# A shared tile's columns: from TensorE transposes to loads in 32x32 blocks and a VectorE transpose

## The chip, the cores and the metric

The kernel runs on one core of a Trainium2 chip. The metric is the device time of one execution in microseconds (us). All arithmetic is fp32; matmuls run on fp32 numbers split into a high and a low part (type fp32r), so that three matmuls of parts stand for one.

## The reference

`x` is (128, 64, 256): 128 samples of 64 rows of 256 numbers. Two stages, each added to its input.

```python
# stage 1, per sample b with type itok[b] (one of the five experts):
s0 = relu(x @ swi[0]) @ swo[0];  s1 = relu(x @ swi[1]) @ swo[1]        # shared, 256 -> 1024 -> 256
eo = relu(x @ wi[itok]) @ wo[itok]                                     # the sample's expert
w  = softmax(relu(concat(eo[:, 0], s0[:, 0], s1[:, 0]) @ g1) @ g2)     # from row 0 of each sample
x  = x + eo * w[:, 0] + s0 * w[:, 1] + s1 * w[:, 2]
# stage 2, a reaction-diffusion step on each sample's 64 x 256 grid, edges reflected:
x  = x + zX * (left - 2x + right) + zY * (up - 2x + down) + zR * x * (1 - x)
```

## The kernel before

**Passes.** The work is cut into passes of 8 chunks (a chunk is 128 of the 1024 hidden columns). Two `PRE` passes compute s0 and s1 for row 0 of each sample, 21 `EXP` passes the experts (a unit is 8 samples with one expert, for 14 big units, or 4 samples, for 7 small ones), and 32 `SH` passes the shared layers: 16 tiles of 8 samples, and for each tile pass b = 0 with the weights swi[0], swo[0] and pass b = 1 with swi[1], swo[1]. A big unit or a tile has 512 columns (128 partitions x 4 rows of x each), a small unit 256. `FIRST` is the first shared pass.

**One loop for all engines.** Every engine walks the same list of chunks g and does its part of it in the order written out there. TensorE does per chunk: transposes if `tile_parts` names some for this chunk, `first_product(g)` (six matmuls into one of three banks `hbank`), and `second_product(g - 2)` (eight matmuls into the four banks `acc`). ScalarE makes the hidden high part `hh` (L781), VectorE the hidden low part `hl` (L471), each after `first_product`; `second_product(g)` waits for the low part, and so does `first_product(g + 3)`, which needs the bank again. A few other steps stand in VectorE's list between them: at a shared tile's odd pass `residual` at chunk 2 and `add_shared(t, 0)` at chunk 3; at the next tile's even pass, for the tile before, `add_shared(t, 1)` at chunk 1, then the stencil: `lap_x`, `react`, `add_x`, `lap_y` at chunk 5 (L539) and `result` at chunk 6. Each engine takes its instructions strictly in this order.

**Columns.** A tile's x lies with rows on partitions (`XS`). The first product wants columns, so TensorE transposes the next tile's x in four 128x128 pieces per half (L656, L657), at chunks 4 and 5 of the pass before, through the bank `tbank`; ScalarE copies the high part (`XH`, L773) and VectorE subtracts for the low part (`XL`, L418).

**Partitions and halos.** In a shared tile partition p * 8 + b holds rows 4p to 4p + 3 of sample b, so the neighbours up and down of a partition's four rows lie 8 partitions away. `halos` (L940 to L946) copies them within SBUF once the tile's sum is complete: two transfers of 120 partitions and two of 8 (the reflected edges). `lap_y` waits for all four.

**SyncE** issues, in this order: the loads of x for unit u + 2 and the stores of unit u - 1 in turns; then the gate's two loads and the first tiles' loads; then for each tile: halos of the tile before, load of x and of the expert's result for tile t + 1, a wait for `result` and the store of the tile before. GpSimd issues the loads of expert weights into `RW`. After the last pass `last_tile` does the stencil of tile 15 in smaller steps, and the halo transfers (L991 to L996) are issued as their rows are ready, in `LAST_ORDER` 0, 3, 1, 2.

Of the kernel before, what the change touches and what calls it, by code (L numbers as in the profile page):

```python
# [5 lines left out]
F32 = mybir.dt.float32  # L6
# [7 lines left out]
NC = F // 128  # L14
# [51 lines left out]
def tile_parts(n, c):  # L66

    if n == 0 or n >= NP - 2 or (PASSES[n][0] == SH and PASSES[n][1] % 2 == 0):
        return []
    tile = tile_of(n) + 1  # L70
    big = tile <= NBIG or tile > NU
    if c == 4:
        return [(tile, 0 if big else None)]
    return [(tile, 1)] if c == 5 and big else []
# [18 lines left out]
XT_ORDER = [key for key in T_ORDER if isinstance(key, tuple)]  # L93
XT_AT = {key: i + 1 for i, key in enumerate(XT_ORDER)}


# [49 lines left out]
def cond_resid_program(nc, x, itok, zx, zy, zr, wi, wo, swi, swo, g1, g2, out):  # L146
    eo_d = nc.dram_tensor("eo_scratch", (NS + NSLOT, S, D), F32, kind="Internal").ap()
    ctx = ExitStack()
    with ctx:
# [10 lines left out]
        HL = sb("hl", [128, NH, 512], F32R)  # L160
        XH = [sb(f"xh{i}", [128, 2, 512], F32R) for i in range(2)]
        XL = [sb(f"xl{i}", [128, 2, 512], F32R) for i in range(2)]
        XF = sb("xf", [128, 2, 128])
# [70 lines left out]
        w_lo = sem("w_lo")  # L234
        w_lo_pool = sem("w_lo_pool")
        x_in = [sem(f"x_in{i}") for i in range(2)]
        eo_out = [sem(f"eo_out{i}") for i in range(2)]
# [10 lines left out]
        halo_in = [sem(f"halo_in{i}") for i in range(2)]  # L248
        o_out = [sem(f"o_out{i}") for i in range(2)]

        def col(a):
# [38 lines left out]
        def out_rows(a, t):  # L290
            return a[8 * t:8 * t + 8, :, :].rearrange("b (p j) d -> p b (j d)", j=4)

# [17 lines left out]
        def _(e):  # L310
# [99 lines left out]
            def tile_low(tile, k):  # L410

                hi, lo = XH[tile % 2], XL[tile % 2]
                e.wait_ge(t_hi, XT_AT[tile, k])
                if k is None:
                    e.tensor_tensor(lo[:, :, 0:256], tbank[:].rearrange("p (k n) -> p k n", k=2),
                                    hi[:, :, 0:256].bitcast(F32), ALU.subtract).then_inc(t_free, 1)
                else:
                    e.tensor_tensor(lo[:, k, :], tbank[:], hi[:, k, :].bitcast(F32),  # L418
                                    ALU.subtract).then_inc(t_free, 1)

            def gate_masks():
# [145 lines left out]
            for g in range(G + LAG):  # L567
# [58 lines left out]
        def _(e):  # L626
# [41 lines left out]
            def first_product(g):  # L668
# [15 lines left out]
                wh, wl, _ = weights(n)  # L684
                xh, xl = XH[tile % 2], XL[tile % 2]
                if c == 0:
                    e.wait_ge(t_free, T_AT[tile_last(tile)])
                if c % 4 == 0:
                    e.wait_ge(*cut_done(weight_set(n), c // 4))
                cs = slice(c * 128, (c + 1) * 128)  # L690
                for k in range(2):
                    e.matmul(bank[:, 0:w], wh[:, k, cs], xh[:, k, 0:w], start=(k == 0), stop=False)  # L692
                    e.matmul(bank[:, 0:w], wh[:, k, cs], xl[:, k, 0:w], start=False, stop=False)  # L693
                    i = e.matmul(bank[:, 0:w], wl[:, k, cs], xh[:, k, 0:w], start=False, stop=(k == 1))  # L694
                i.then_inc(h_prod, 1)
# [65 lines left out]
        def _(e):  # L761
            e.dma_start(itk[:], col(itok)).then_inc(itok_in, 16)

            def tile_high(tile, k):
                hi = XH[tile % 2]
# [55 lines left out]
            for g in range(G + LAG):  # L821
                n, c = CHUNKS[g] if g < G else (NP, g - G)
                if g < G:
                    for tile, k in tile_parts(n, c):
                        tile_high(tile, k)
                if (n, c) == (FIRST + 1, 0):
                    e.wait_ge(dve_seq, AT["minus max"])
# [18 lines left out]
        def _(e):  # L846
# [9 lines left out]
                            pattern=[[-1, 128]], channel_multiplier=1).then_inc(consts, 1)  # L856
            e.iota(b8[:], [[0, 16], [1, 8]], base=0, channel_multiplier=0,
                   allow_small_or_imprecise_dtypes=True).then_inc(consts, 1)
# [40 lines left out]
        def _(e):  # L899
# [90 lines left out]
            e.wait_ge(dve_seq, AT["last", 3])  # L990
            e.dma_start(y[8:128, 0, :], y[0:120, 4, :]).then_inc(halo_in[t % 2], 16)  # L991
            e.dma_start(y[0:120, 5, :], y[8:128, 1, :]).then_inc(halo_in[t % 2], 16)
            e.wait_ge(dve_seq, AT["last", 1])
            e.dma_start(y[0:8, 0, :], y[0:8, 2, :]).then_inc(halo_in[t % 2], 16)
            e.wait_ge(dve_seq, AT["last", 2])
            e.dma_start(y[120:128, 5, :], y[120:128, 3, :]).then_inc(halo_in[t % 2], 16)  # L996
            for a in range(2):
                e.wait_ge(dve_seq, AT["result", t, a])
                e.dma_start(out_rows(out, t)[:, :, 2 * a * D:(2 * a + 2) * D],
                            OT[t % 2][:, 2 * a:2 * a + 2, :].rearrange("p j d -> p (j d)")).then_inc(o_out[t % 2], 16)  # L1000
# [23 lines left out]
```

## Time and profile before

| | |
|---|---|
| median of 3 runs | 1192.12 us (1191.96 to 1195.7) |
| the profiled execution | 1192.88 us, span 1191.0 us |
| TensorE busy | 1164.8 us, 98%, clock 0.995 of full |
| VectorE, ScalarE, GpSimd busy | 672.7, 460.2, 72.5 us |
| DMA, mean over the span | 82 GB/s |
| one hidden high part on ScalarE (L781, 128x512) | 0.60 us |
| one hidden low part on VectorE (L471, 128x512) | 0.69 us |

Busy matmul time is modelled and matmuls overlap, so how close TensorE is to its limit is read from the times at which matmuls start, not from 98%. A wait on another engine matters only where the chain of work that ended last goes through it. A DMA share is the busy share of the core's 16 DMA engines (1.00 is all of them).

### The profile page before, as it was taken

Reading aid. Unit: us, or ns where it says so; the run is one execution under the profiler, and the core shown is the slowest. Engines: PE = TensorE matmul, PEld = TensorE weight load, DVE = VectorE, ACT = ScalarE, POOL = GpSimd, SP = SyncE. Lnnn points to the kernel's source line nnn. Section 1 sums busy time; section 2 is a strip of 40 time slices with the busy share of each in tenths; the row PEclk is TensorE's granted clock in tenths of the full one; section 3 lists DMA queues with packets and bytes.
Section 4 is the critical chain, followed back from the end, with each engine's and each line's share of the span. In section 5 each row is a group of like instructions: output and inputs, shape, how many; then the busy total and the mean of one; then the engine's idle time right before and its main releaser. Section 6 shows DMA issues by size and latency. Waiting matters only on the chain.

```text
span 1191.0 us, 16700 instructions
## 1 busy us (share of the span) xinstructions
PE 1164.8 (98%) x6124; PEld 992.0 (83%) x6124; DVE 672.7 (56%) x1008; ACT 460.2 (39%) x802; POOL 72.5 (6%) x105
## 2 busy tenths in 40 slices
PE   5999999999999999999999999999999999999995
PEld 4888888888889998888888888888888888888884
DVE  6655555555557763555555565465465465465455
ACT  3445444444545652332423333333333233333232
POOL 3101110110112200000000000000000000000001
PEclk9999999999999999999999999999999999999998
DMA  7644453444446633022022022021021021021110
GB/s 230 182 124 129 145 152 111 145 148 129 118 140 187 218 109 93 10 54 62 5 58 63 1 62 54 9 63 45 18 62 45 18 63 45 18 63 36 27 27 27
DMA packets 39041, 98.09 MB, mean 82 GB/s; under 512 B 8368, under 2 KB 15536, under 8 KB 38960
## 3 DMA queue, kind: packets, MB, share of 16 engines
q1 hardware_dynamic: 26720, 52.98, 16.3%
q0 software_dynamic: 12096, 44.05, 12.5%
q8 instruction: 49, 0.80, 0.3%
q14 instruction: 32, 0.26, 0.1%
q10 hardware_dynamic: 144, 0.00, 0.0%
HBM read 75.24 MB, written 17.56 MB: 78 GB/s over the span
## 4 chain that ended last, share of the span: by engine, by line
PE 95%; DVE 2%; DMA 1%; SPq 1%; issue 0%; ACT 0%; DVEq 0%; ACTq 0%
PE acc L717 31%; PE acc L718 15%; PE hbank L693 15%; PE hbank L692 15%; PE hbank L694 15%; PE tbank L656 2%; DMA g1s<-in_L_cond_g 1%; PE tbank L657 1%; DMA xs<-in_x 0%; SPq L915 0%; SPq L903 0%; PE acc L706 0%; PE tbank L664 0%; DVE rows L350 0%; DMA itk<-in_itok_B 0%
## 5 line engine op out<-in xcount | busy, mean ns | idle before, releaser
L471 DVE SCALAR_TENSOR_TENSOR hl<-hbank,hh 128x512 fp32r<-128x512 f32 (+1 forms) x424 | 278.0, 656 | 437.9 <-ACT hh L781 437.7
L781 ACT ACTIVATE hh<-hbank 128x512 fp32r<-128x512 f32 (+1 forms) x424 | 241.6, 570 | 621.0 <-PE hbank L694 617.3
L717 PE MATMUL acc<-swo,hh 128*128 128x512 f32 x1024 | 370.9, 396 | 0.0
L718 PE MATMUL acc<-swo,hl 128*128 128x256 f32 x1024 | 286.9, 280 | 0.0
L717 PEld LDWEIGHTS acc<-swo,hh 128*128 128x128 f32 x1024 | 192.3, 188 | 45.5 <-DVE eo L489 0.2
L717 PE MATMUL acc<-ewo,hh 128*128 128x512 f32 x560 | 205.1, 397 | 0.2
L692 PE MATMUL hbank<-xh,swh 128*128 128x512 f32 x512 | 204.8, 400 | 0.0
L693 PE MATMUL hbank<-xl,swh 128*128 128x512 f32 x512 | 202.2, 395 | 0.0
L718 PEld LDWEIGHTS acc<-swo,hl 128*128 128x128 f32 x1024 | 193.1, 189 | 10.0
L694 PE MATMUL hbank<-xh,swl 128*128 128x512 f32 x512 | 199.7, 390 | 0.0
L718 PE MATMUL acc<-ewo,hl 128*128 128x256 f32 x560 | 157.3, 281 | 0.0
L717 PEld LDWEIGHTS acc<-ewo,hh 128*128 128x128 f32 x560 | 105.2, 188 | 23.9 <-issue 1.2
L692 PE MATMUL hbank<-xh,ewh 128*128 128x512 f32 (+1 forms) x336 | 122.6, 365 | 0.0
L694 PE MATMUL hbank<-xh,ewl 128*128 128x512 f32 (+1 forms) x336 | 119.6, 356 | 0.0
L693 PE MATMUL hbank<-xl,ewh 128*128 128x512 f32 (+1 forms) x336 | 119.3, 355 | 0.0
L692 PEld LDWEIGHTS hbank<-xh,swh 128*128 128x128 f32 x512 | 96.2, 188 | 22.4
L694 PEld LDWEIGHTS hbank<-xh,swl 128*128 128x128 f32 x512 | 96.2, 188 | 22.1
L718 PEld LDWEIGHTS acc<-ewo,hl 128*128 128x128 f32 x560 | 105.2, 188 | 4.8
L693 PEld LDWEIGHTS hbank<-xl,swh 128*128 128x128 f32 x512 | 96.2, 188 | 10.7
L692 PEld LDWEIGHTS hbank<-xh,ewh 128*128 128x128 f32 x336 | 63.2, 188 | 11.0 <-issue 0.2
L694 PEld LDWEIGHTS hbank<-xh,ewl 128*128 128x128 f32 x336 | 63.0, 188 | 9.1
L693 PEld LDWEIGHTS hbank<-xl,ewh 128*128 128x128 f32 x336 | 63.4, 189 | 5.0
(164 smaller groups left out, 873.7 us busy)
## 6 DMA issues: line engine op xcount, KB each, us to landing
rw<-in_L_cond_wi POOLq DMA_DIRECT2D x42, 512.0 KB, 4.4
rw<-in_L_cond_wo POOLq DMA_DIRECT2D x42, 512.0 KB, 5.3
xs<-in_x SPq DMA_DIRECT2D x140, 64.0 KB, 2.9
eo_scratch<-eo SPq DMA_DIRECT2D x140, 64.0 KB, 2.7
xs<-in_x SPq DMA_DIRECT2D x16, 512.0 KB, 5.2
ei<-eo_scratch SPq DMA_DIRECT2D x16, 512.0 KB, 6.6
out<-ot SPq DMA_DIRECT2D x15, 512.0 KB, 3.8
y<-y SPq DMA_DIRECT2D x32, 120.0 KB
```

What stands on the lines that cost most here:

```text
L471: e.scalar_tensor_tensor(HL[:, g % NH, 0:w], bank[:, 0:w], 0.0, HH[:, g % NH, 0:w].bitcast(F32), ALU.max, ALU.subtract).then_inc(h_lo, 1)
L656: e.transpose(tbank[:, j * 128:(j + 1) * 128], src[:, j, k * 128:(k + 1) * 128], ident[:])
L657: e.transpose(tbank[:, 384:512], src[:, 3, k * 128:(k + 1) * 128], ident[:]).then_inc(t_prod, 1)
L692: e.matmul(bank[:, 0:w], wh[:, k, cs], xh[:, k, 0:w], start=(k == 0), stop=False)
L693: e.matmul(bank[:, 0:w], wh[:, k, cs], xl[:, k, 0:w], start=False, stop=False)
L694: i = e.matmul(bank[:, 0:w], wl[:, k, cs], xh[:, k, 0:w], start=False, stop=(k == 1))
L717: e.matmul(acc[j][:, 0:2 * D], HH[:, g % NH, js], woc[:, c, :], start=(c == 0), stop=False)
L718: m = e.matmul(acc[j][:, D:2 * D], HL[:, g % NH, js], woc[:, c, 0:D], start=False, stop=last)
L781: e.activation(HH[:, g % NH, 0:w], hbank[g % HRING][:, 0:w], ACT.Relu).then_inc(h_hi, 1)
```

## The change

A shared tile's columns no longer come from TensorE. `load_tile_blocks` loads x again, in 16 DMAs of 32 partitions per tile, so that each 32x32 block lands at its transposed place (rows still on partitions inside the block); VectorE's `transpose` turns the blocks in one instruction (`turn_tile`, 128x1024), ScalarE copies the high part of the whole tile (`tile_high_whole`) and VectorE subtracts for the low part (`tile_low_whole`). `XH` and `XL` of a shared tile hold (row j, half k, 128), so the first product reads four runs of 128. Partition order of a shared tile is sample by sample, partition 16 b + p, so neighbours lie 1 partition away, the large halo transfers have 127 partitions, and the reflected edges (8 partitions each, 16 apart) overwrite parts of them and wait for them. SyncE's order: the first tile's blocks ahead of a unit's store, each later tile's after the halos and ahead of its x.

```diff
@@
 def tile_parts(n, c):
 
-    if n == 0 or n >= NP - 2 or (PASSES[n][0] == SH and PASSES[n][1] % 2 == 0):
+    if n == 0 or n >= FIRST - 1:
         return []
     tile = tile_of(n) + 1
-    big = tile <= NBIG or tile > NU
+    big = tile <= NBIG
...
+def next_tile(n, c):
+
+    if c != 4 or n < FIRST - 1 or n >= NP - 2:
+        return None
+    if n == FIRST - 1:
+        return 0
+    t, b = PASSES[n][1] // 2, PASSES[n][1] % 2
+    return t + 1 if b == 1 else None
...
+        XB, XZ = RW[0:2], RW[2]
+
+        def unit_cols(a):
+            return a[:].rearrange("p (k n) -> p k n", k=2)
+
+        def tile_cols(a, k):
+            return a[:].rearrange("p (j k n) -> p j k n", j=4, k=2)[:, :, k, :]
...
-            return a[8 * t:8 * t + 8, :, :].rearrange("b (p j) d -> p b (j d)", j=4)
+            return a[8 * t:8 * t + 8, :, :].rearrange("b (p j) d -> (b p) (j d)", j=4)
...
+            def turn_tile(t):
+
+                if t == 0:
+                    e.wait_ge(*cut_done(1 + NU, 2))
+                else:
+                    e.wait_ge(xt_lo, t)
+                e.wait_ge(xb_in[t % 2], 256 * (t // 2 + 1))
+                e.transpose(XZ[:], XB[t % 2][:]).then_inc(xz_done, 1)
+
+            def tile_low_whole(t):
+                tile = 1 + NU + t
+                e.wait_ge(xt_hi, t + 1)
+                e.tensor_tensor(XL[tile % 2][:], XZ[:], XH[tile % 2][:].bitcast(F32), ALU.subtract).then_inc(xt_lo, 1)
...
                 if g < G:
                     for tile, k in tile_parts(n, c):
                         tile_low(tile, k)
+                    if next_tile(n, c) is not None:
+                        turn_tile(next_tile(n, c))
+                    if next_tile(n, c - 1) is not None:
+                        tile_low_whole(next_tile(n, c - 1))
...
+                    xh, xl = ([tile_cols(a[tile % 2], k) for k in range(2)] for a in (XH, XL))
+                    to = bank[:].rearrange("p (j n) -> p j n", j=4)
+                    if c == 0:
+                        e.wait_ge(xt_lo, PASSES[n][1] // 2 + 1)
...
+            def tile_high_whole(t):
+                tile = 1 + NU + t
+                e.wait_ge(xz_done, t + 1)
+                e.wait_ge(h_prod, (LAST_PASS[tile - 2] + 1) * NC)
+                e.activation(XH[tile % 2][:], XZ[:], ACT.Copy).then_inc(xt_hi, 1)
...
             def load_tile_x(t):
                 tile = 1 + NU + t
-                e.wait_ge(t_prod, T_AT[tile_last(tile - 2)])
-                if t >= 2:
+                if t < 2:
+                    e.wait_ge(t_prod, T_AT[tile_last(tile - 2)])
+                else:
                     e.wait_ge(dve_seq, AT["residual", t - 2])
                 e.dma_start(XS[tile % 2][:].rearrange("p j d -> p (j d)"), out_rows(x, t)).then_inc(x_in[tile % 2], 16)
...
+            def load_tile_blocks(t):
+
+                if t == 0:
+                    e.wait_ge(*cut_done(1 + NU, 0))
+                if t == 1:
+                    e.wait_ge(*cut_done(1 + NU, 1))
+                if t >= 2:
+                    e.wait_ge(xz_done, t - 1)
+                to = XB[t % 2][:].rearrange("p (j n) -> p j n", n=128)
+                for q in range(4):
+                    rows = x[8 * t + 2 * q:8 * t + 2 * q + 2, :, :].rearrange("b (m j) (k d) -> (b m) (j k) d", j=4, k=2)
+                    for a in range(4):
+                        e.dma_start(to[32 * a:32 * a + 32, :, 32 * q:32 * q + 32],
+                                    rows[:, :, 32 * a:32 * a + 32]).then_inc(xb_in[t % 2], 16)
...
             def halos(t):
                 y = Y[t % 2]
                 e.wait_ge(dve_seq, AT["shared", t, 1])
-                e.dma_start(y[8:128, 0, :], y[0:120, 4, :]).then_inc(halo_in[t % 2], 16)
-                e.dma_start(y[0:120, 5, :], y[8:128, 1, :]).then_inc(halo_in[t % 2], 16)
-                e.dma_start(y[0:8, 0, :], y[0:8, 2, :]).then_inc(halo_in[t % 2], 16)
-                e.dma_start(y[120:128, 5, :], y[120:128, 3, :]).then_inc(halo_in[t % 2], 16)
+                e.dma_start(y[1:128, 0, :], y[0:127, 4, :]).then_inc(halo_in[t % 2], 16)
+                e.dma_start(y[0:127, 5, :], y[1:128, 1, :]).then_inc(halo_in[t % 2], 16)
+
+            def reflected(t):
+
+                y = Y[t % 2]
+                e.wait_ge(halo_in[t % 2], 64 * (t // 2) + 32)
+                e.dma_start(y[0:128:16, 0, :], y[0:128:16, 2, :]).then_inc(halo_in[t % 2], 16)
+                e.dma_start(y[15:128:16, 5, :], y[15:128:16, 3, :]).then_inc(halo_in[t % 2], 16)
...
                     load_tile_x(0)
+                if u == NU - 1:
+                    load_tile_blocks(0)
                 if u >= 1:
                     store_unit(u - 1)
...
             load_tile_x(1)
+            load_tile_blocks(1)
             load_tile_eo(1)
             for t in range(1, NT):
                 halos(t - 1)
+                reflected(t - 1)
                 if t + 1 < NT:
+                    load_tile_blocks(t + 1)
                     load_tile_x(t + 1)
                     load_tile_eo(t + 1)
...
             e.wait_ge(dve_seq, AT["last", 3])
-            e.dma_start(y[8:128, 0, :], y[0:120, 4, :]).then_inc(halo_in[t % 2], 16)
-            e.dma_start(y[0:120, 5, :], y[8:128, 1, :]).then_inc(halo_in[t % 2], 16)
+            e.dma_start(y[1:128, 0, :], y[0:127, 4, :]).then_inc(halo_in[t % 2], 16)
+            e.dma_start(y[0:127, 5, :], y[1:128, 1, :]).then_inc(halo_in[t % 2], 16)
             e.wait_ge(dve_seq, AT["last", 1])
-            e.dma_start(y[0:8, 0, :], y[0:8, 2, :]).then_inc(halo_in[t % 2], 16)
             e.wait_ge(dve_seq, AT["last", 2])
-            e.dma_start(y[120:128, 5, :], y[120:128, 3, :]).then_inc(halo_in[t % 2], 16)
+            reflected(t)
```

## Rows read from the trace of the kernel before

**Rows 1.** The page, chain that ended last: shares of the span by engine.

```profile
PE 95%; DVE 2%; DMA 1%; SPq 1%; issue 0%; ACT 0%; DVEq 0%; ACTq 0%
```

**Rows 2.** Timeline of TensorE, shared stage: start us, duration us, engine, line.

```profile
530.34 0.49 PE L656 MATMUL tbank<-ident,xs 128*128 128x128 f32 x3
...
533.57 0.40 PE L692 MATMUL hbank<-xh,swh 128*128 128x512 f32 x1
...
536.35 0.40 PE L692 MATMUL hbank<-xh,swh 128*128 128x512 f32 x1
```

**Rows 3.** Instructions on tbank: line, count, duration ns min/median/max, first and last start.

```profile
L657 PE MATMUL tbank<-ident,xs x60: 272/273/421, 31.0 to 1121.9; 128*128 128x128 f32 x60
```

**Rows 4.** Timeline of ScalarE, a high part of 128x1024 copied in SBUF.

```profile
429.96 1.05 ACT L811 ACTIVATE ewh<-rw 128x1024 fp32r<-128x1024 f32 x1
```

**Rows 5.** Timelines of VectorE and TensorE at one shared tile's Laplacian and next sum.

```profile
555.90 1.22 DVE L539 TENSOR_TENSOR ss<-y 128x1024 f32<-128x1024 f32 x1
558.08 0.69 DVE L471 SCALAR_TENSOR_TENSOR hl<-hbank,hh 128x512 fp32r<-128x512 f32 x1 [0.96 <-ACT hh L781]
...
572.62 1.21 DVE L516 TENSOR_TENSOR y<-y,eo 128x1024 f32<-128x1024 f32 x1
...
562.82 0.39 PE L717 MATMUL acc<-swo,hh 128*128 128x512 f32 x1
```

**Rows 6.** DMA view: packets; queues; issues: count, KB each, median us to landing.

```profile
DMA packets 39041, 98.09 MB, mean 82 GB/s; under 512 B 8368, under 2 KB 15536, under 8 KB 38960
...
q10 hardware_dynamic: 144, 0.00, 0.0%
...
rw<-in_L_cond_wi POOLq DMA_DIRECT2D x42, 512.0 KB, 4.4
...
xs<-in_x SPq DMA_DIRECT2D x140, 64.0 KB, 2.9
...
y<-y SPq DMA_DIRECT2D x32, 120.0 KB
...
y<-y SPq DMA_DIRECT2D x32, 8.0 KB
...
g2s<-in_L_cond_g SPq DMA_DIRECT2D x1, 3.0 KB, 1.8
```

**Rows 7.** Windows: stretch, length, busy per engine (count), PEclk, DMA share, GB/s.

```profile
549.00:550.00 1.00, 1.00 (x8) 0.87 (x7) 0.76 (x3) 0.60 (x1) 0.00 (x0) 1.00 0.45 123
553.00:554.00 1.00, 1.00 (x6) 0.83 (x5) 1.00 (x2) 0.00 (x0) 0.00 (x0) 1.00 0.74 242
```

**Rows 8.** Timeline of SyncE's queue behind one shared tile's sum.

```profile
547.69 0.92 SPq L943 DMA_DIRECT2D y<-y  x1
...
549.54 0.68 SPq L945 DMA_DIRECT2D y<-y  x1
...
551.03 0.62 SPq L933 DMA_DIRECT2D xs<-in_x  x1
```

**Rows 9.** Windows, then timelines of TensorE, SyncE and VectorE at the end.

```profile
31.00:34.40 3.40, 3.40 (x17) 2.81 (x16) 0.89 (x2) 1.11 (x3) 0.00 (x0) 0.55 0.31 82
...
1182.00:1183.00 1.00, 0.00 (x0) 0.00 (x0) 1.00 (x2) 0.12 (x1) 0.77 (x2) 0.50 0.45 120
...
1177.80 0.28 PE L718 MATMUL acc<-swo,hl 128*128 128x256 f32 x1
...
1179.57 0.86 SPq L991 DMA_DIRECT2D y<-y  x1
...
1184.81 1.23 DVE L539 TENSOR_TENSOR ss<-y 128x1024 f32<-128x1024 f32 x1
```

**Rows 10.** Timelines of SyncE, VectorE and TensorE in the last unit's pass.

```profile
425.40 29.72 SPq L925 DMA_DIRECT2D eo_scratch<-eo  x12
...
438.83 0.42 DVE L471 SCALAR_TENSOR_TENSOR hl<-hbank,hh 128x256 fp32r<-128x256 f32 x1 [1.25 <-ACT hh L781]
...
443.55 0.40 PE L717 MATMUL acc<-ewo,hh 128*128 128x512 f32 x1
```

More of the change, by code:

```diff
@@ L160, in cond_resid_program @@
         HL = sb("hl", [128, NH, 512], F32R)
-        XH = [sb(f"xh{i}", [128, 2, 512], F32R) for i in range(2)]
-        XL = [sb(f"xl{i}", [128, 2, 512], F32R) for i in range(2)]
+        XH = [sb(f"xh{i}", [128, 1024], F32R) for i in range(2)]
+        XL = [sb(f"xl{i}", [128, 1024], F32R) for i in range(2)]
         XF = sb("xf", [128, 2, 128])
@@ L235, in cond_resid_program @@
         w_lo_pool = sem("w_lo_pool")
+        xb_in = [sem(f"xb_in{i}") for i in range(2)]
+        xz_done = sem("xz_done")
+        xt_hi = sem("xt_hi")
+        xt_lo = sem("xt_lo")
         x_in = [sem(f"x_in{i}") for i in range(2)]
@@ L410, in tile_low @@
             def tile_low(tile, k):
-                hi, lo = XH[tile % 2], XL[tile % 2]
+                hi, lo = unit_cols(XH[tile % 2]), unit_cols(XL[tile % 2])
                 e.wait_ge(t_hi, XT_AT[tile, k])
@@ L684, in first_product @@
                 wh, wl, _ = weights(n)
-                xh, xl = XH[tile % 2], XL[tile % 2]
-                if c == 0:
-                    e.wait_ge(t_free, T_AT[tile_last(tile)])
+                if PASSES[n][0] == EXP:
+                    xh, xl = ([unit_cols(a[tile % 2])[:, k, 0:w] for k in range(2)] for a in (XH, XL))
+                    to = bank[:, 0:w]
+                    if c == 0:
+                        e.wait_ge(t_free, T_AT[tile_last(tile)])
+                else:
+                    xh, xl = ([tile_cols(a[tile % 2], k) for k in range(2)] for a in (XH, XL))
+                    to = bank[:].rearrange("p (j n) -> p j n", j=4)
+                    if c == 0:
+                        e.wait_ge(xt_lo, PASSES[n][1] // 2 + 1)
                 if c % 4 == 0:
@@ L691, in first_product @@
                 for k in range(2):
-                    e.matmul(bank[:, 0:w], wh[:, k, cs], xh[:, k, 0:w], start=(k == 0), stop=False)
-                    e.matmul(bank[:, 0:w], wh[:, k, cs], xl[:, k, 0:w], start=False, stop=False)
-                    i = e.matmul(bank[:, 0:w], wl[:, k, cs], xh[:, k, 0:w], start=False, stop=(k == 1))
+                    e.matmul(to, wh[:, k, cs], xh[k], start=(k == 0), stop=False)
+                    e.matmul(to, wh[:, k, cs], xl[k], start=False, stop=False)
+                    i = e.matmul(to, wl[:, k, cs], xh[k], start=False, stop=(k == 1))
                 i.then_inc(h_prod, 1)
@@ L764, in tile_high @@
             def tile_high(tile, k):
-                hi = XH[tile % 2]
+                hi = unit_cols(XH[tile % 2])
                 e.wait_ge(t_prod, T_AT[tile, k])
@@ L825, in _ @@
                         tile_high(tile, k)
+                    if next_tile(n, c) is not None:
+                        tile_high_whole(next_tile(n, c))
                 if (n, c) == (FIRST + 1, 0):
@@ L856, in _ @@
                             pattern=[[-1, 128]], channel_multiplier=1).then_inc(consts, 1)
-            e.iota(b8[:], [[0, 16], [1, 8]], base=0, channel_multiplier=0,
+            e.iota(b8[:], [[1, 8], [0, 16]], base=0, channel_multiplier=0,
                    allow_small_or_imprecise_dtypes=True).then_inc(consts, 1)
@@ L929, in load_tile_x @@
                 tile = 1 + NU + t
-                e.wait_ge(t_prod, T_AT[tile_last(tile - 2)])
-                if t >= 2:
+                if t < 2:
+                    e.wait_ge(t_prod, T_AT[tile_last(tile - 2)])
+                else:
                     e.wait_ge(dve_seq, AT["residual", t - 2])
                 e.dma_start(XS[tile % 2][:].rearrange("p j d -> p (j d)"), out_rows(x, t)).then_inc(x_in[tile % 2], 16)
+            def load_tile_blocks(t):
[11 more added lines that the diff above has]
+                                    rows[:, :, 32 * a:32 * a + 32]).then_inc(xb_in[t % 2], 16)
             def load_tile_eo(t):
@@ L990, in _ @@
             e.wait_ge(dve_seq, AT["last", 3])
-            e.dma_start(y[8:128, 0, :], y[0:120, 4, :]).then_inc(halo_in[t % 2], 16)
-            e.dma_start(y[0:120, 5, :], y[8:128, 1, :]).then_inc(halo_in[t % 2], 16)
+            e.dma_start(y[1:128, 0, :], y[0:127, 4, :]).then_inc(halo_in[t % 2], 16)
+            e.dma_start(y[0:127, 5, :], y[1:128, 1, :]).then_inc(halo_in[t % 2], 16)
             e.wait_ge(dve_seq, AT["last", 1])
-            e.dma_start(y[0:8, 0, :], y[0:8, 2, :]).then_inc(halo_in[t % 2], 16)
             e.wait_ge(dve_seq, AT["last", 2])
-            e.dma_start(y[120:128, 5, :], y[120:128, 3, :]).then_inc(halo_in[t % 2], 16)
+            reflected(t)
             for a in range(2):
                 e.wait_ge(dve_seq, AT["result", t, a])
-                e.dma_start(out_rows(out, t)[:, :, 2 * a * D:(2 * a + 2) * D],
+                e.dma_start(out_rows(out, t)[:, 2 * a * D:(2 * a + 2) * D],
                             OT[t % 2][:, 2 * a:2 * a + 2, :].rearrange("p j d -> p (j d)")).then_inc(o_out[t % 2], 16)
```

## The prediction, made before the changed kernel ran

> **What bounds the kernel now.** I read first the page's chain of work that ended last, then TensorE's timeline over one shared tile, then the timelines of VectorE and SyncE beside it, then the windows for what the DMAs do meanwhile. The chain is 95% TensorE [rows 1]: matmuls follow each other without a gap, and every other engine runs behind them. So time can come off in one way only, by taking work off TensorE, and time is added wherever another engine hands over later than the matmuls can wait. In the shared stage a chunk (six matmuls of the first product, eight of the second) starts every 2.78 us, and 3.23 us after the last one where four 128x128 transposes stand in front of it [rows 2]. The reader is to see two numbers there: 0.45 us is the price of a group of four transposes, 2.78 us the beat by which lateness is counted.
>
> **The change, part by part.**
>
> *Transposes leave TensorE.* The kernel has 60 full groups of four [rows 3]; 14 big units have two each, so 28, and 16 shared tiles the other 32. 32 x 0.45 = 14.4 us, all of it on the path. The matmuls that stay are the same in number and columns; the first product now reads its 512 columns as four runs of 128 that lie 256 apart. No row shows a moving operand in runs. Below, it costs nothing; above, each run could cost as much as a 128-column transpose, 0.45 for four, instead of the 0.23 us that one of six matmuls has of half a beat; 0.22 us x 1536 (32 passes x 48) = 338 us. I take nothing, since the rows with 512, 256 and 128 columns all go by columns; the far end gets 2 chances in 100 and is outside the range.
>
> *VectorE and ScalarE.* Per tile VectorE loses two subtractions of 0.69 us and gains a transpose and a subtraction of 128x1024; a VectorE instruction of 128x1024 in fp32 takes 1.22 us [rows 5]. ScalarE swaps two copies of 0.60 us (the length of its hidden high parts too) for one of 1.05 us [rows 4]. I take 1.22 for the transpose, whose price no row shows: nothing at the least, 2.5 us at the most (twice that of the same shape). What covers it: at chunk 4 of the odd pass VectorE is done with the tile's sum at 573.84, 572.62 and 1.22 [rows 5]; transpose 1.22, high part 1.05, hidden high 0.60, hidden low 0.69 end at 577.4, and TensorE wants that chunk's low half after two more beats and the first product of a third, at about 579.7 (572.75 + 2 x 2.78 + half a beat). 2.3 us are left, so even 2.5 us for the transpose hides; without that cover each microsecond would cost 15 us in all.
>
> *The halos.* The partitions are now sample by sample, so the two large halo transfers go from 120 to 127 partitions, and the two small ones (8 partitions) wait for them, with SyncE standing still. How many DMA engines share a transfer can be counted. Every engine that takes part leaves one 4-byte completion. The packets under 512 B are 8368 [rows 6]: 84 GpSimd loads x 16 = 1344; the other queue 144; the three 128-element columns 384; the 12-byte rows of the last SyncE row 256; that leaves 6240. SyncE's issues add up to 408 (23 rows of this view less the GpSimd and ScalarE ones, the first and the last shown); at 16 each that would be 6528. 288 are missing, which is 32 x 1 + 32 x 8: the 120-partition transfers ran on 15 engines, the 8-partition ones on 8, all others on 16. Each is an equal share per engine (8 partitions, 1 partition); sixteen unequal shares of 7 and 8 were there to be had for 120 and weren't taken. 127 can be cut equally only into one share. So I take it that both transfers of 127 KB run on one engine, and on the same one. By the Trainium skill, DMA: Bandwidth & Descriptors, section Why a DMA increments its semaphore by 16 and not by 1, a hardware-queue transfer takes the largest number up to 16 that divides both sides' slowest dimension, and 127 partitions give 1; the counts of this trace agree with it at 120 and 8, and no run yet shows 127.
>
> The price of a packet of 1 KB: in 549 to 550 us the share 0.45 of 16 engines moved the 123 KB of one halo, 7.2 engine-us for 120 packets, 60 ns; in 553 to 554 the share 0.74 moved 242 KB, 49 ns per KB [rows 7]. Alone on its engine a transfer meets no other, so I take the faster as 50 ns. 254 packets: 12.7 us (15.2 at 60).
>
> Let H be the first halo's issue, 547.69 [rows 8]. Its packets begin about 1.3 us later (none before 549, 0.45 in the next microsecond [rows 7]). Then 12.7 us, 0.2 for the semaphore, 0.7 for the first small issue [rows 8], and 1.8 from the second one's issue to its landing (the landing time of the smallest transfer, [rows 6]): H + 16.7 (H + 19.2 at 60 ns). The y Laplacian read the halos at 555.90 [rows 5], H + 8.2, and hidden low of the next chunk is queued behind it on VectorE; TensorE wants that one at 562.82 [rows 5], by which 1.22 + 0.69 + 0.05 of VectorE must be over, so the Laplacian can start as late as 560.86, H + 13.15. The stall of TensorE is 16.7 - 13.15 = 3.55 us per tile (6.1 at 60 ns), for 15 tiles 53 us (91). It comes again each tile, since the next H follows TensorE.
>
> *The clock.* A pause costs more if the clock falls. TensorE ended at 1178.1, its last matmul begins at 1177.80 [rows 9], and 1182 to 1183 was granted 0.50, the 1.2 GHz level; after the pause before 30.7 us, 3.4 us were granted 0.55 [rows 9]. A low stretch of 3.4 us costs about 1.7 us. Between 1178.1 and 1182 there is about as much time as in a pause of 3.55 us, so few of these should bring the fall: I take 2 or 3 of the 15, 4 us; all of them at 60 ns, 25 us.
>
> *Block loads.* 16 more DMAs of SyncE per tile, in packets of 128 B, 256 per engine. An x load's issue took 0.62 us [rows 8], so 16 take 9.9. They stand behind the small halos: SyncE is free at about H + 15, the last is issued at H + 25 and lands at H + 27 to 29. The transpose wants them at 573.84, which is H + 26.2, plus the stall of 3.55, plus 2.3 of cover: H + 32. They cost nothing. Were the packet as dear as 60 ns, 256 of them take 15.4 us and end at H + 32: the edge. At 0.92 us an issue (the odd halo's [rows 8]) they end at H + 32 too.
>
> *The first tile.* Its blocks are issued behind the store that begins at 425.40 (four DMAs, until 428.5 at some 0.75 each, register load and issue) and before the next unit's store: 9.9 us, to 438.4, landed by about 441. VectorE is at chunk 4's place at 439.25, and TensorE wants that chunk's low half at 443.55 [rows 10]; 441 + 1.22 + 1.05 + 0.39 + 0.42 is 444.1 (the last two are the half as wide hidden high and low). I take 0.5 us, none at the least, 6 at the most (0.92 us an issue). The next unit's store slips from 437 to 438.4; the gate's loads hang on the last unit's store and don't move.
>
> *The tail.* After the last matmul the small halos were issued as soon as their rows were there and the Laplacian began at 1184.81 [rows 9]. Now H is 1179.57 and it begins at H + 16.7 = 1196.3: 11.5 us (14 at 60 ns).
>
> **Sum.** Against the profiled execution, 1192.88 us with a span of 1191.0 (1.9 us lie around it; the median of the runs shown, 1192.12, is 0.8 less): -14.4 + 53 + 4 + 0.5 + 11.5 = +54.6, 1247.5; taken off the median 1246.7. I say 1248. With 60 ns: -14.4 + 91 + 25 + 4 + 14 = +120, 1312. Below 50 ns no row goes, but an engine by itself may: each nanosecond less is 0.25 us per tile, and at 46 ns the stalls, the clock and the tail come to 21 us less, 1227.
>
> **The rivals.**
>
> *The halos spread over 15 or 16 engines, which is faster than before.* If shares may be unequal (8 partitions on fifteen engines and 7 on one, which the counts at 120, 8 each on fifteen, and 8, 1 each on eight, don't exclude), the large halos land by H + 4.2, the small ones by H + 7, in time for H + 13.15; SyncE begins its blocks at H + 6. In the tail the small ones land at about 1185.5, 0.7 after the Laplacian began before. -14.4 + 0.5 + 0.7: 1180. For it: 120 fits. Against it: no transfer of this trace has unequal shares. It decides from the engines on which a 127-partition transfer runs: if two share it, 254 x 50 / 2 = 6.4 us and the small halos land at H + 10.4, the stall is gone. Chance 0.13.
>
> *The blocks come late too.* The 128 B packets take as long as 1 KB ones, or an issue 0.9 us, and the halo's stall adds: the transpose waits 1 to 3 us per tile beyond its cover, 15 x 2 = 30 us, 1278. For it: they are issued behind the halos; against: 12-byte packets landed in 1.8 us [rows 6]. Chance 0.12. The skill's page DMA: Bandwidth & Descriptors, Specifications, says that below 512 B a transfer falls off line rate; no row here has packets of 128 B, and by that rule this rival's first term is the likely one.
>
> *The first products pay for reading four stretches*: over 1320. Chance 0.03. That the change leaves the transposes where they are can't be: they aren't issued.
>
> **How the numbers follow.** Forecast 0.70 (1225 to 1312 with its own bounds), late blocks 0.12, spread halos 0.13, dear first products 0.03, rest 0.02. The time is the forecast's, 1248. The range is 1222 to 1318: it leaves out the spread halos, the dear first products and some of the ends, about 0.2. Within 0.3% (3.6 us, about what a measurement of this kernel can tell from no change) needs a stall that happens to equal the gain: 0.02. Faster 0.13, slower 0.85.
>
> **What would show it.** Groups of tbank transposes 28 instead of 60, and chunks of 2.78 us throughout: the gain. Per shared tile one pause of TensorE of some 3.5 us, with the Laplacian on VectorE waiting for a y transfer, and in the windows a DMA share near 0.06 for 12 us after H: one engine. Packets under 512 B: the large halos give 1 completion each instead of 15. In the tail, the Laplacian 11 us later. If the windows show the halo's bytes within a microsecond or two, the equal shares were wrong and the time is near 1180; if the pause is there but stands before the transpose of blocks, it is the second rival.

## The result and the profile after

The changed kernel takes 1251.8 us, median of four runs (1248.41 to 1255.13), against 1192.05 us for the kernel before: 1.0493 times as long, 95% interval [1.0454, 1.0532]. The forecast was 1248, the range 1222 to 1318. The profiled execution took 1248.41 us with a span of 1246.6, 55.6 more than before. It was the fastest of the four, and the account below is of this one; by the medians the loss is 59.7.

The page of the changed kernel: span, packets, chain that ended last, then the group of the y Laplacian (busy us, mean ns, then idle time before it and what ended it), one group of DMA issues and, from the view of its tbank instructions, the groups of transposes.

```profile
span 1246.6 us, 16639 instructions
...
DMA packets 108450, 106.73 MB, mean 86 GB/s; under 512 B 77552, under 2 KB 84944, under 8 KB 108368
...
PE 67%; DMA 20%; DVE 7%; SPq 3%; issue 1%; ACT 1%; DVEq 0%; ACTq 0%
...
L578 DVE TENSOR_TENSOR ss<-y 128x1024 f32<-128x1024 f32 x16 | 19.6, 1225 | 128.4 <-DMA y<-y 128.4
...
rw<-in_x SPq DMA_DIRECT2D x256, 32.0 KB, 2.2
...
L700 PE MATMUL tbank<-ident,xs x28: 272/273/422, 30.7 to 328.3; 128*128 128x128 f32 x28
```

The chain was 95% TensorE [rows 1]; now a fifth of the span goes through DMAs, and the page's chain by line names them: `y<-y`, the halos. The 28 groups of transposes that are left are those of the big units, as forecast. The packets tell on how many engines a halo runs. The 256 block loads bring 65536 packets of 128 B and 256 x 16 completions; 8368 [rows 6] + 65536 + 4096 = 78000. The view shows 77552, 448 fewer: 32 large halo transfers now leave 1 completion where each left 15, 32 x 14 = 448. A transfer of 127 partitions runs on one engine.

Timelines of the changed kernel around one shared tile: SyncE, VectorE, TensorE (start us, duration us; in brackets idle time before and what ended it).

```profile
550.38 0.72 SPq L1017 DMA_DIRECT2D y<-y  x1
551.14 1.26 SPq L1018 DMA_DIRECT2D y<-y  x1
564.14 0.61 SPq L1024 DMA_DIRECT2D y<-y  x1
...
565.44 10.43 SPq L1006 DMA_DIRECT2D rw<-in_x  x16
...
566.51 1.22 DVE L578 TENSOR_TENSOR ss<-y 128x1024 f32<-128x1024 f32 x1 [7.83 <-DMA y<-y]
567.65 0.68 DVE L510 SCALAR_TENSOR_TENSOR hl<-hbank,hh 128x512 fp32r<-128x512 f32 x1
...
579.44 1.24 DVE L453 STREAM_TRANSPOSE rw<-rw 128x1024 f32<-128x1024 f32 x1
...
568.39 0.50 PE L767 MATMUL acc<-swo,hh 128*128 128x512 f32 x1 [2.71 <-DVE hl L510]
...
597.97 0.71 SPq L1017 DMA_DIRECT2D y<-y  x1
```

H, the issue of the tile's first large halo, is 550.38. SyncE stands still until the large halos have landed (564.14, H + 13.8), issues the reflected edges, and the Laplacian starts at H + 16.13, where it started at H + 8.2 before [rows 5, 8]. The hidden low part is queued behind it, and TensorE waits. H to H is 47.59 us; it was 45.48, and of that 0.90 were transposes: 47.59 = 45.48 - 0.90 + 3.0. The pause of TensorE costs 3.0 us a tile.

Windows of the changed kernel (stretch, length, busy time of PE, PEld, DVE, ACT, POOL with counts, clock, DMA share, GB/s): the halo's flight; a stretch in which the clock fell; the tail.

```profile
551.40:563.40 12.00, 12.00 (x62) 10.14 (x61) 5.17 (x7) 3.10 (x6) 0.00 (x0) 1.00 0.07 23
757.00:765.00 8.00, 6.38 (x19) 5.29 (x19) 4.18 (x6) 0.75 (x2) 0.00 (x0) 0.57 0.32 49
1226.00:1239.00 13.00, 0.00 (x0) 0.00 (x0) 4.12 (x6) 1.20 (x2) 2.38 (x5) 0.61 0.06 20
```

A share of 0.07 is one engine of sixteen (0.0625), busy without a gap, and it moves 23 GB/s. In the kernel before, one microsecond of the halo's flight moved 123 GB/s [rows 7].

**Where the 55.6 us are**, by SyncE's starts of the first large halo of each tile: the first H comes 0.56 later than before, the last 45.66 later, the end 55.6 later. Up to the first H, 1.8 of transposes went and about 2.4 came at the first tile (below). The 15 periods between are 45.1 longer: 15 pauses of 2.99 (44.9), less 14 x 0.90 of transposes (12.6), and 12.9 in six periods that are longer than the rest (0.1 is rounding).

```profile
740.63 0.71 SPq L1017 DMA_DIRECT2D y<-y  x1
...
790.92 0.71 SPq L1017 DMA_DIRECT2D y<-y  x1
...
840.03 0.71 SPq L1017 DMA_DIRECT2D y<-y  x1
```

These three starts are 50.29 and 49.11 apart, 2.7 and 1.5 over the 47.57 of their neighbours, and in both the clock was low after the pause (0.57 above for the first; 1.2 and 2.4 GHz mixed). The tail gives 9.9.

### The profile page after: what moved, and what is told of

Its sections match the earlier page's. It is cut to its first block, busy times and chain, and to the rows that moved or that the text cites. A ratio compares the mean times of both kernels' runs of the same rounds, so it can differ in the third digit from the quotient of the medians.

```text
span 1246.6 us, 16639 instructions
## 1 busy us (share of the span) xinstructions
PE 1167.1 (94%) x5996; PEld 987.9 (79%) x5996; DVE 683.3 (55%) x1008; ACT 455.8 (37%) x786; POOL 72.4 (6%) x105
## 2 busy tenths in 40 slices
DMA packets 108450, 106.73 MB, mean 86 GB/s; under 512 B 77552, under 2 KB 84944, under 8 KB 108368
## 4 chain that ended last, share of the span: by engine, by line
PE 67%; DMA 20%; DVE 7%; SPq 3%; issue 1%; ACT 1%; DVEq 0%; ACTq 0%
PE acc L767 22%; DMA y<-y 19%; PE acc L768 11%; PE hbank L743 11%; PE hbank L742 11%; PE hbank L744 11%; DVE hl L510 2%; DVE eo L528 2%; DVE ss L578 2%; DVE y L555 1%; SPq L1017 1%; SPq L1006 1%; ACT hh L837 1%; SPq L1024 1%; PE tbank L699 1%
## 5 line engine op out<-in xcount | busy, mean ns | idle before, releaser
L767 PE MATMUL acc<-swo,hh 128*128 128x512 f32 x1024 | 379.7, 404 | 40.7 <-DVE hl L510 40.7
L768 PE MATMUL acc<-swo,hl 128*128 128x256 f32 x1024 | 290.8, 284 | 0.0
L767 PEld LDWEIGHTS acc<-swo,hh 128*128 128x128 f32 x1024 | 196.1, 191 | 92.7 <-DVE hl L510 47.1
L768 PEld LDWEIGHTS acc<-swo,hl 128*128 128x128 f32 x1024 | 197.4, 193 | 9.7
L578 DVE TENSOR_TENSOR ss<-y 128x1024 f32<-128x1024 f32 x16 | 19.6, 1225 | 128.4 <-DMA y<-y 128.4
L742 PEld LDWEIGHTS hbank<-xh,ewh 128*128 128x128 f32 x336 | 63.3, 188 | 11.1 <-issue 0.3
```

Source lines behind the costliest of these rows:

```text
L578: e.tensor_tensor(SS[:], y[:, 0:4, :], y[:, 2:6, :], ALU.add).then_inc(*V.up())
L742: e.matmul(to, wh[:, k, cs], xh[k], start=(k == 0), stop=False)
L767: e.matmul(acc[j][:, 0:2 * D], HH[:, g % NH, js], woc[:, c, :], start=(c == 0), stop=False)
L768: m = e.matmul(acc[j][:, D:2 * D], HL[:, g % NH, js], woc[:, c, 0:D], start=False, stop=last)
```

## The experiments

**1. The large halos cut to suit more engines.** `spread_112_15`, with the counts of the waits raised to match; the same in the tail.

```diff
-                e.dma_start(y[1:128, 0, :], y[0:127, 4, :]).then_inc(halo_in[t % 2], 16)
-                e.dma_start(y[0:127, 5, :], y[1:128, 1, :]).then_inc(halo_in[t % 2], 16)
+                e.dma_start(y[1:113, 0, :], y[0:112, 4, :]).then_inc(halo_in[t % 2], 16)
+                e.dma_start(y[113:128, 0, :], y[112:127, 4, :]).then_inc(halo_in[t % 2], 16)
+                e.dma_start(y[0:112, 5, :], y[1:113, 1, :]).then_inc(halo_in[t % 2], 16)
+                e.dma_start(y[112:127, 5, :], y[113:128, 1, :]).then_inc(halo_in[t % 2], 16)
```

> The changed kernel with each 127-partition halo cut into one of 112 and one of 15 partitions (which should run on 16 and 15 engines instead of 1), all waits kept. Theory (the halos ran on one engine, 254 packets at 47 ns): no pause of TensorE before the Laplacian, no clock fall in the shared stage, Laplacian at H + 8.2, time 1192 - 14.4 + 3 (first tile) + 1 (tail) = 1181 to 1183. Rival (the reflected halos' wait in SyncE's queue, or the block loads behind them, is what costs): 1240 or more, Laplacian still several us late. Second rival (first products or transposes cost part of it): between 1190 and 1230 with no DMA wait at the Laplacian.

Measured: 1183.41 us (0.4 above the expected range), 0.9916 [0.9902, 0.9929] of the kernel before. The packets on this kernel's page:

```profile
DMA packets 109410, 106.73 MB, mean 90 GB/s; under 512 B 78512, under 2 KB 85904, under 8 KB 109328
```

Timelines of its SyncE, VectorE and TensorE:

```profile
594.01 0.57 SPq L1017 DMA_DIRECT2D y<-y  x1
...
598.55 0.62 SPq L1026 DMA_DIRECT2D y<-y  x1
...
602.22 1.22 DVE L578 TENSOR_TENSOR ss<-y 128x1024 f32<-128x1024 f32 x1
...
530.43 0.40 PE L742 MATMUL hbank<-xh,swh 128*128 128x512 f32 x1
...
533.21 0.40 PE L742 MATMUL hbank<-xh,swh 128*128 128x512 f32 x1
...
536.00 0.40 PE L742 MATMUL hbank<-xh,swh 128*128 128x512 f32 x1
```

78512 - 77552 = 960 = 32 x (16 + 15 - 1): the pieces run on 16 and 15 engines. The large halos have landed at H + 4.5, the Laplacian of the shared tiles waits for no DMA, and H to H is 44.59, 45.48 less two groups of transposes (the last period is 40.64, and was 40.65). So the halos' single engine is what made the change a loss; the rest of it is a net gain. The chunks shown start 2.78 and 2.79 us apart, so the reads in four runs cost nothing.

**2. A number of engines between one and sixteen.** The same four lines cut at 122 + 5 (`two_engines_122_5`) and at 125 + 2 (`five_engines_125_2`). The number of instructions is that of experiment 1, only the engines differ.

```diff
-                e.dma_start(y[1:113, 0, :], y[0:112, 4, :]).then_inc(halo_in[t % 2], 16)
+                e.dma_start(y[1:123, 0, :], y[0:122, 4, :]).then_inc(halo_in[t % 2], 16)
```

> Halos cut into 122 and 5 partitions. By the divisor reading 122 = 2 x 61 runs on 2 engines and 5 on 5: 61 packets per engine and transfer, 122 x 47 ns = 5.8 us, Laplacian wanted at H + 8.2 starts at about H + 10.5, inside the cover that ends at H + 13.15, so TensorE doesn't pause: 1183 to 1187, the tail 4 to 5 us longer than with 112 and 15. Completions: 2 + 5 per halo. If unequal shares were possible (16 engines), it is 1182 and the tail is short. If the cover is smaller than I worked out, TensorE pauses and it is over 1195.

> Halos cut into 125 and 2 partitions. Divisor reading: 125 on 5 engines, 2 on 2; 50 packets per engine, 2.4 us for both halos; completions of 4 bytes per tile 2 x (5 + 2) for the large ones. Time 1182 to 1185. If the engines were the partitions over 8 rounded up, it would be 16 completions for 125 and 1 for 2.

Measured: 1187.64 us (0.6 above the expected range), 0.9952 [0.9937, 0.9967], and 1183.89 us, 0.992 [0.9902, 0.9938]. The packets, a line that reads the same in the pages of both kernels:

```profile
DMA packets 108642, 106.73 MB, mean 90 GB/s; under 512 B 77744, under 2 KB 85136, under 8 KB 108560
```

Timelines of SyncE and VectorE with 122 + 5, then the row of its waits (us in total, times, longest):

```profile
593.27 0.74 SPq L1017 DMA_DIRECT2D y<-y  x1
...
601.30 0.62 SPq L1026 DMA_DIRECT2D y<-y  x1
...
1179.37 1.22 DVE L578 TENSOR_TENSOR ss<-y 128x1024 f32<-128x1024 f32 x1 [5.28 <-DMA y<-y]
```
```profile
DVE ss L578 <- DMA y<-y: 38.1, 16, 5.3
```

SyncE with 125 + 2:

```profile
593.39 0.86 SPq L1017 DMA_DIRECT2D y<-y  x1
...
598.62 0.63 SPq L1026 DMA_DIRECT2D y<-y  x1
```

77744 - 77552 = 192 = 32 x (2 + 5 - 1): a transfer of 122 partitions takes 2 engines, one of 5 takes 5 (in the other kernel 5 and 2). The sum is 7 in both kernels; the times tell which piece has which: the large halos have landed at H + 8.0 with 122 + 5 and at H + 5.2 with 125 + 2. With 122 + 5 the Laplacian waits some 2.2 us in each shared tile and starts at about H + 10.4, and TensorE doesn't wait: the cover behind H + 8.2 is real, here as far as H + 10.4 (experiment 6 goes to its edge). Most of what 122 + 5 loses against 112 + 15 is in the tail, which has no cover: 15.7 us from the last H to the end instead of 11.8. By the Trainium skill, DMA: Bandwidth & Descriptors, section Why a DMA increments its semaphore by 16 and not by 1, the count is the largest number up to 16 that divides both sides' slowest dimension; the packets agree at 127 (1), 122 (2), 125 (5) and 112 (16).

**3. The tail by itself.** `tail_only`: the changed kernel, with only the last tile's halos cut 112 + 15.

> Only the last tile's halos are cut into 112 and 15; the 15 others stay at 127. Theory: the stalls and clock falls of the shared stage stay, the tail's 10.9 us less about 0.7 go: 10 us faster than the changed kernel, 1239 to 1243. If the tail were hidden otherwise: no difference, 1251.

Measured: 1245.49 us, 2.5 above the expected range, 1.042 [1.0391, 1.045]; the ratio is 0.73% of 1192 less, 8.7 us. From the last H to the end of the span it took 11.8 us, 21.4 in the changed kernel: 9.55 less, as expected. VectorE of this kernel, then a window:

```profile
1238.12 1.22 DVE L578 TENSOR_TENSOR ss<-y 128x1024 f32<-128x1024 f32 x1 [1.41 <-DMA y<-y]
```
```profile
569.00:577.00 8.00, 6.57 (x19) 5.44 (x20) 4.18 (x6) 0.94 (x2) 0.00 (x0) 0.57 0.33 52
```

The rest is the clock. The shared stage is the same program as in the changed kernel, with the same pauses, but in this profiled execution the clock fell after eight of the 15 pauses and not after six, the first time at 569.7 and not at 757.9: first to last H takes 4.3 us more. The first tile's pause brought a fall too, and the first H is 2.1 later: -9.55 + 4.3 + 2.1 is -3.15, and the spans, 1243.4 and 1246.6, differ by 3.2. So the number of falls isn't fixed by the pauses.

**4. The clock.** `filler`: the changed kernel with eight matmuls of no use ahead of those that wait, in each tile's pause.

```diff
+                if FIRST + 2 < n < NP and PASSES[n][1] % 2 == 1 and c == 0:
+                    for _ in range(8):
+                        e.matmul(tbank[:], SWH[0][:, 0, 0:128], SWH[0][:, 0, 0:512], start=True, stop=True)
```

> The changed kernel with 8 matmuls of 512 columns (1.86 us) into the unused bank tbank before the second product that pauses, per tile; their result is read by nobody. TensorE pauses 3.0 us there, so they fit into the pause. Theory (some 11 us of the loss are low clock after pauses): the clock stays full in the shared stage and the time falls by about 11 us, to 1240. Rival (the falls of the clock cost nothing, or the pauses alone aren't what brings them): same time as the changed kernel or, if the filler doesn't fit, up to 28 us more.

Measured: 1237.55 us, 1.0358 [1.0341, 1.0376]: adding work made it 14 us faster by the medians. TensorE's timeline and a window of this kernel:

```profile
567.50 1.98 PE L809 MATMUL tbank<-swh 128*128 128x512 f32 x8
570.36 0.50 PE L767 MATMUL acc<-swo,hh 128*128 128x512 f32 x1 [0.89 <-DVE hl L510]
```
```profile
757.00:765.00 8.00, 7.13 (x35) 5.71 (x34) 4.94 (x7) 1.95 (x5) 0.00 (x0) 1.00 0.25 41
```

The window that had a clock of 0.57 has 1.00, and H to H is 47.53 to 47.62 (the last period is 43.61, and was 45.17): the 50.3 and 49.1 are gone. The pause itself is as long as before (0.89 idle is left behind 1.98 of filler), so the wait and the clock are told apart. In its profiled execution the 12.9 us of long periods are gone, and the first H is 2.0 later, behind the first tile's pause, which has no filler (446 to 450 was granted 0.63, and 1.00 in the changed kernel's execution): -12.9 + 2.0 is -10.9, and the spans, 1235.5 and 1246.6, differ by 11.1.

**5. Is the loss in the old partition order too?** `old_113_7`: the kernel before, its 120-partition halos cut to 113 + 7, so that one engine has 226 packets of the large pieces. One edit to the kernel before, no block loads, no transpose, the small halos in their old place without a wait.

```diff
-                e.dma_start(y[8:128, 0, :], y[0:120, 4, :]).then_inc(halo_in[t % 2], 16)
-                e.dma_start(y[0:120, 5, :], y[8:128, 1, :]).then_inc(halo_in[t % 2], 16)
+                e.dma_start(y[8:121, 0, :], y[0:113, 4, :]).then_inc(halo_in[t % 2], 16)
+                e.dma_start(y[121:128, 0, :], y[113:120, 4, :]).then_inc(halo_in[t % 2], 16)
+                e.dma_start(y[0:113, 5, :], y[8:121, 1, :]).then_inc(halo_in[t % 2], 16)
+                e.dma_start(y[113:120, 5, :], y[121:128, 1, :]).then_inc(halo_in[t % 2], 16)
```

> The kernel before, transposes on TensorE and all, with each 120-partition halo cut into 113 (a prime, so one engine) and 7 partitions, nothing waiting that didn't wait before. 228 packets at 47.3 ns on one engine: 10.8 us, Laplacian at H + 12.3, inside the cover that ends at H + 13.15: no pause of TensorE in the 15 tiles; the tail 7 us longer: 7 us slower than before, 1199 to 1200. If the cover is smaller, 15 pauses show: over 1205. If one engine isn't what makes halos slow: no difference from before.

> The same, and the two 8-partition halos wait for the large ones in SyncE's queue, as in the changed kernel. Laplacian at H + 12.2 + 0.1 + 2.4 = H + 14.7: TensorE pauses 1.55 us per tile, 23 us, tail 9.4 us longer, few or no falls of the clock: 33 us slower than before, about 1226. If SyncE's wait costs nothing by itself, it equals the kernel without the order.

(`old_113_7_ordered` has besides, ahead of the small halos, `e.wait_ge(halo_in[t % 2], 96 * (t // 2) + 64)`.) Measured: 1233.12 us, 1.0334 [1.0317, 1.0352], and 1238.81 us, 1.0369 [1.0351, 1.0386]. Both expectations were missed, the first by 33 us and the second by 13. Timelines of SyncE and VectorE and three windows of the first:

```profile
600.21 0.74 SPq L943 DMA_DIRECT2D y<-y  x1
...
602.68 4.40 SPq L946 DMA_DIRECT2D y<-y  x1
...
608.59 0.62 SPq L933 DMA_DIRECT2D xs<-in_x  x1
609.26 0.60 SPq L938 DMA_DIRECT2D ei<-eo_scratch  x1
...
615.34 1.23 DVE L539 TENSOR_TENSOR ss<-y 128x1024 f32<-128x1024 f32 x1 [6.84 <-DMA y<-y]
```
```profile
603.00:608.00 5.00, 5.00 (x26) 4.17 (x26) 3.14 (x4) 1.19 (x2) 0.00 (x0) 1.00 0.08 24
610.00:613.00 3.00, 3.00 (x17) 2.56 (x16) 0.00 (x0) 0.81 (x2) 0.00 (x0) 1.00 1.01 252
615.50:616.80 1.30, 0.00 (x1) 0.00 (x0) 1.30 (x2) 0.60 (x1) 0.00 (x0) 1.00 0.06 25
```

SyncE and VectorE of `old_113_7_ordered`:

```profile
599.75 0.74 SPq L943 DMA_DIRECT2D y<-y  x1
...
615.08 1.23 DVE L539 TENSOR_TENSOR ss<-y 128x1024 f32<-128x1024 f32 x1 [7.04 <-DMA y<-y]
```

In `old_113_7` the Laplacian starts at H + 15.1 and not at H + 12.3. Until 608 the one engine works alone at 24 GB/s. Then the next tile's two loads are issued, from 610 on all engines are busy (share 1.01), and the halo packets still to come start 83 ns apart (12 in a microsecond, in the trace's packet records) instead of 47. The theory put to the test: the loads delay the halo. In the changed kernel SyncE stood waiting then, so its loads couldn't do that.

The expectation of the next run words it as taking turns on the halo's engine, and the packet records say otherwise. From 610 to 613 the halo's own packets took a median of 86 ns, against 46 before; their times add up to 1.14 engines, so there was no room for load packets between them. The loads' 4 KB packets add up to the other 15 engines, and the last 10 of them start 156 ns apart when the halo is over, with the share of one engine (0.06 above): its part of the loads, done last. So the halo isn't interrupted; each of its packets is slower while the other engines are busy. What they share isn't shown.

**6. The test of that theory.** `old_113_7_loads_wait`: the next tile's loads wait for the halos.

```diff
+                    e.wait_ge(halo_in[(t - 1) % 2], 96 * ((t - 1) // 2 + 1))
```

> The kernel before with halos of 113 and 7, and the next tile's loads of x and eo (2 x 512 KB) wait until the halos have landed; without that it took 1233.1, with the Laplacian at H + 15.1 instead of the H + 12.3 expected. Theory (the two big loads, which run at a share of 1.00 from H + 10 on, took turns with the last halo packets on the one engine): Laplacian at H + 12.5 to 12.9, no pause of TensorE, 1200 to 1202. Rival (SyncE's fourth issue, 4.4 us long, or the one engine itself sets H + 15): no difference, 1233.

Measured: 1200.99 us, 1.0059 [1.0043, 1.0076]. SyncE and VectorE:

```profile
594.16 0.74 SPq L943 DMA_DIRECT2D y<-y  x1
...
596.63 4.39 SPq L946 DMA_DIRECT2D y<-y  x1
...
607.28 0.62 SPq L933 DMA_DIRECT2D xs<-in_x  x1
607.29 1.23 DVE L539 TENSOR_TENSOR ss<-y 128x1024 f32<-128x1024 f32 x1 [4.83 <-DMA y<-y]
```

The Laplacian comes 0.2 later than expected, but H + 13.13 is just inside the cover of H + 13.15: TensorE has no pause, and 32 us are gone by waiting longer with a load. That the loads delay the halo is shown by taking them away. The rival is out: the fourth issue is as long as before, 4.39 us. `old_113_7_ordered` has no loads beside its halos either, since SyncE waits; its small halos come behind the wait instead, as in the changed kernel, the Laplacian starts at H + 15.3, 2.2 past the cover, and H to H is 47.65, 2.2 over 45.48.

**7. The first tile and the block loads.** `two_queues`: experiment 1, and half of the first tile's block loads issued by GpSimd. `no_blocks`: experiment 1 with all block loads left out (the transposed data is whatever lies there).

```diff
+            for q in range(2, 4):
...
+                for a in range(4):
+                    e.dma_start(to[32 * a:32 * a + 32, :, 32 * q:32 * q + 32],
+                                rows[:, :, 32 * a:32 * a + 32]).then_inc(xg_in, 16)
...
-                for q in range(4):
+                for q in range(2 if t == 0 else 4):
```

> The kernel with halos of 112 and 15, and in it half of the first tile's 16 block loads issued by GpSimd, whose queue is empty by then, instead of SyncE. Theory: the 2.6 us pause of TensorE in the last unit's pass comes from SyncE's 11 us of issues; with half of them elsewhere the blocks land some 4 us earlier and the pause goes: 2 to 3 us faster than the kernel with halos of 112 and 15, 1180 to 1181. Rival (the transfer of small packets itself is late, not the issue): no difference.

> The kernel with halos of 112 and 15, the 256 block loads left out and with them the wait for them (VectorE transposes what lies in the buffer, so the shared layers' sums are of other numbers). If the block loads cost nothing but the first tile's pause (2.6 us), it is as fast as the kernel that splits the first tile's issues over two queues, 1180 to 1181. If their 65536 packets of 128 B slow other transfers or SyncE on the path, it is faster than 1178.

Measured: 1180.57 us, 0.9888 [0.9871, 0.9904], and 1178.68 us, 0.9875 [0.9859, 0.9892]. SyncE and VectorE of the changed kernel, then VectorE of `two_queues`:

```profile
428.92 11.41 SPq L1006 DMA_DIRECT2D rw<-in_x  x16
...
442.05 1.25 DVE L453 STREAM_TRANSPOSE rw<-rw 128x1024 f32<-128x1024 f32 x1 [3.10 <-DMA rw<-in_x]
```
```profile
439.20 1.23 DVE L456 STREAM_TRANSPOSE rw<-rw 128x1024 f32<-128x1024 f32 x1
```

With two queues no wait stands ahead of the first transpose, and the span is 1176.8, 14.2 less than before, nearly all of the 14.4 that the transposes cost (by the medians, 13.5: the kernel before took 1194.02 beside it). The block loads cost nothing outside the first tile: H to H is 44.59 with and without them, the spans are 1176.8 and 1176.9, and the intervals overlap. The 1178.68 us fall between the two expectations; the spans decide.

**8. The tail's order.** `tail_order`: `two_queues`, the last tile's upward halos issued as soon as their own rows are ready.

```diff
+            e.wait_ge(dve_seq, AT["last", 0])
+            e.dma_start(y[0:112, 5, :], y[1:113, 1, :]).then_inc(halo_in[t % 2], 16)
+            e.dma_start(y[112:127, 5, :], y[113:128, 1, :]).then_inc(halo_in[t % 2], 16)
             e.wait_ge(dve_seq, AT["last", 3])
```

> The two-queue kernel, and in the last tile the halo pair that reads row 0 is issued as soon as block 0 is there, one block (0.97 us) ahead of the pair that reads row 3. The Laplacian waited 1.4 us for the halos there. Theory: about 0.9 us faster than the two-queue kernel's 1180.6, near the limit of what can be told; if SyncE isn't what holds the tail, no difference.

Measured: 1178.15 us, 0.9875 [0.9859, 0.9892], 1.2% under the kernel before and 5.9% under the changed one. Against `two_queues` the intervals overlap; the traces show the gain: span 1175.8 against 1176.8, the last period 39.67 us instead of 40.62, and the tail's Laplacian waits 0.4 us instead of 1.4.

## Why the prediction was right

**One engine: right.** The counts of before (120 on 15, 8 on 8) were enough to tell 127 from them, and the rival of spread halos, which had 0.13, is out: 77552 packets, share 0.07.

**Price of a packet: 50 ns taken, 47 measured.** The 254 packets took 11.8 us, 12.7 were predicted. Landing came at H + 13.8 and the small halos followed as worked out, H + 16.13 against H + 16.7. So a pause of 2.98 us, and 44.9 us for 15 tiles instead of 53. Taking the slower end, 60 ns, would have missed by 60 us. The faster row was taken because the transfer would be alone on its engine; that this row also had the busier engines is no reason, since packets beside busy engines were slower, not faster (experiment 5).

**Cover to H + 13.15: right.** (560.86 is H + 13.17; the difference is nothing here.) 16.13 - 13.15 is the pause of 2.98. `old_113_7`, at H + 15.13, should pause by 1.98: its periods have a median of 47.5, 2.0 over 45.48. At H + 13.13 there is no pause.

**Transposes, 14.4 us: right.** H to H without pauses is 44.59, 0.89 less, and `two_queues` has 14.2 of it in its span. VectorE's transpose took 1.24 us (1.22 taken), and the first products' reads in runs cost nothing.

**The clock: the term mis-sized.** "I take 2 or 3 of the 15, 4 us" was six falls and 12.9 us. Three of them cost 2.8 and three 1.5, where I took 1.7 each. `filler` shows that the idle time of TensorE brings them, not the halo: the same wait, no falls in the tiles. The size was taken from one stretch after a longer wait early in the kernel [rows 9]; how often a pause of 3 us brings a fall was guessed from a single pause at the end, and the same pauses brought eight falls in `tail_only`.

**First tile: 0.5 predicted, some 2.4 measured.** SyncE's 16 issues took 11.41 us, not 9.9: 0.71 each instead of the x load's 0.62 [rows 8], and they began at 428.92. The price of an issue was read from a load of another shape. It stayed below its bound of 6.

**Tail: 11.5 predicted; the Laplacian comes 10.9 later, the end 9.9 later.**

**Late blocks: out.** They land 2.2 us after issue, and no transpose but the first tile's waits for them.

Sum by what was measured in the profiled execution: -14.4 + 44.9 + 12.9 + 2.4 + 9.9 = 55.7, against 55.6. Against the median 4.1 more are missing; whether they are more falls of the clock isn't shown. The mechanism was right, but that the forecast of +54.6 comes so near is luck: the pauses (8 too many) and the clock (9 too few) cancel.

## What to carry to other kernels

Count the DMA engines of a transfer in the packets under 512 B before its partition count is changed: 120 to 127 partitions, 6% more bytes, made it a one-engine transfer, and two more instructions (112 + 15) made it fast. Read a wait by the time to which it is covered: 8 us of lateness cost 3, and with one engine more a shared tile lost nothing. And a transfer on few engines is at the mercy of whatever is issued behind it; a wait in the queue may be what protects it.

## What the runs showed of the hardware

- One engine moving 1 KB packets within SBUF starts one each 47 ns alone, and each 83 ns while two full-width loads keep the other 15 busy (252 GB/s in sum): the packets themselves take 86 ns instead of 46. One engine alone with 4 KB load packets starts one each 156 ns.
- Pauses of TensorE of 3.0 us every 47.6 us: the granted clock fell after six of 15 in one execution and after eight of 15 in another (`tail_only`), in pairs of following tiles, and not after the others. Why after these stays open. With 0.9 us left of each pause it fell after none. With pauses of 2.0 us (`old_113_7`) two of 14 periods were long (49.1).
- An issue on SyncE can block: that of a 7-partition halo took 4.40 us behind a one-engine transfer (4.39 in the two kernels made from it), 0.64 for the one before it. What it waited for isn't shown.
- 16 loads of 32 KB in packets of 128 B, issued in 10.4 us, ran unnoticed beside the matmuls.
